# Two Transformer layers with a mixture of experts on one core: the routing step and two softmax steps put in another order

## The reference, cut to what matters

```python
x = x + softmax(layernorm_gamma_beta(sim(layernorm(x), ctx)))     # attention, layer 0
x = x + moe(layernorm(x))                                         # feed forward, layer 0
x = x + softmax(mask(scores(ctx, ctx) * layernorm(x)))            # attention, layer 1
x = x + down(silu(gate(layernorm(x))) * up(layernorm(x)))         # feed forward, layer 1

# moe: 8 experts, the best 2 of each token, at most 160 tokens of each choice for an expert
logits = xt @ gate_w;  top_p, top_i = top_k(softmax(logits), 2)
for k in range(2):
    pos = position of the token among those that chose the expert as choice k
    out += keep * w * (gelu(buf @ w1 + b1) @ w2 + b2 + gelu(buf @ wd) @ wu)
out += 0.2 * (gelu(xt @ sw1 + sb1) @ sw2 + sb2 + gelu(xt @ swd) @ swu)      # shared expert
```

## Time and profile before

| what | value |
|---|---|
| time, median of 3 runs | 301.19 us (301.11 to 302.14) |
| the profiled execution's own time | 304.5 us |
| its span | 302.7 us |
| TensorE busy | 290.1 us, 96% of the span |
| VectorE busy | 243.2 us, 80% |
| ScalarE busy | 155.2 us, 51% |
| GpSimd busy | 116.3 us, 38% |
| chain that ended last | PE 69%, DVE 11%, ACT 7%, DMA 5%, POOL 4% |

### The profile page before, as it was taken

How to read it: one execution, slowest core, us unless ns; L and a number is a source line. 1 busy time by engine, 2 the same in 40 slices (tenths; PEclk the granted TensorE clock), 3 DMA queues, 4 the chain that set the end, 5 groups by cost and what they waited for, 6 DMA issues and landing times.

```text
span 302.7 us, 5910 instructions
## 1 busy us (share of the span) xinstructions
PE 290.1 (96%) x1931; PEld 251.9 (83%) x1931; DVE 243.2 (80%) x647; ACT 155.2 (51%) x369; POOL 116.3 (38%) x144
## 2 busy tenths in 40 slices
PE   8988999969999999999999999999999899999895
PEld 6545688859898998989899888999888699999795
DVE  4888878848998988889888899898974778796733
ACT  2677985415554655646556555655533634535210
POOL 7527410351328074380834706051051215442431
PEclk9999999999999999999999999999999999999999
DMA  7933206550949448293573926446034000010102
GB/s 214 333 137 88 90 0 191 176 173 2 299 166 260 175 83 305 61 298 128 133 253 69 326 93 168 171 79 226 1 43 141 0 3 0 0 36 1 36 1 70
DMA packets 21858, 38.07 MB, mean 126 GB/s; under 512 B 3147, under 2 KB 12427, under 8 KB 21836
## 3 DMA queue, kind: packets, MB, share of 16 engines
q1 hardware_dynamic: 17356, 32.55, 32.6%
q0 software_dynamic: 4480, 5.25, 9.2%
HBM read 31.37 MB, written 6.42 MB: 125 GB/s over the span
## 4 chain that ended last, share of the span: by engine, by line
PE 69%; DVE 11%; ACT 7%; DMA 5%; POOL 4%; issue 3%; SPq 0%; DVEq 0%; POOLq 0%; ACTq 0%
PE hb L811 25%; PE yb L830 24%; PE yb L845 5%; PE hb L959 4%; PE tb L711 4%; DVE bst L1231 1%; POOL rstd L472 1%; DMA xg<-xnorm_dram,row_of 1%; DMA x<-xacc_dram 1%; DVE xn L1237 1%; PE rb L976 1%; DMA xacc_dram<-ysb,third_row 1%; PE yb L959 1%; ACT sm L1024 1%; DMA projw<-projw_dram 1%
## 5 line engine op out<-in xcount | busy, mean ns | idle before, releaser
L830 PE MATMUL yb<-raw,h 128*128 128x256 f32 x384 | 96.5, 379 | 1.4 <-ACT h L1137 1.4
L830 PEld LDWEIGHTS yb<-raw,h 128*128 128x128 f32 x384 | 69.1, 189 | 8.8 <-ACT h L1137 1.8
L1137 ACT ACTIVATE h<-hb,b 128x320 f32<-128x320 f32 (+1 forms) x80 | 44.6, 558 | 58.4 <-PE hb L811 57.1
L811 PE MATMUL hb<-xT_hi,w_hi 128*128 128x320 f32 (+1 forms) x180 | 71.2, 396 | 0.5 <-ACT small L1141 0.5
L811 PE MATMUL hb<-xT_lo,w_hi 128*128 128x320 f32 (+1 forms) x180 | 58.7, 326 | 0.0
L811 PE MATMUL hb<-xT_hi,w_lo 128*128 128x320 f32 (+1 forms) x180 | 58.6, 326 | 0.0
L573 POOL DMA_INDIRECT xacc_dram<-ysb,row_of x16 | 28.2, 1764 | 78.5 <-ACT ysb L1004 76.0
L1263 DVE COPY_PREDICATED pick<-bits,pick 128x544 int32<-128x544 uint8 x56 | 43.3, 773 | 0.6
L557 POOL DMA_INDIRECT xg<-xnorm_dram,row_of x24 | 28.7, 1196 | 32.5 <-DVE row_of L1535 16.3
L1648 DVE TENSOR_TENSOR w_lo<-raw,w_hi 128x256 fp32r<-128x256 f32 x84 | 34.5, 415 | 6.6 <-ACT w_hi L1004 6.5
L811 PEld LDWEIGHTS hb<-xT_hi,w_hi 128*128 128x128 f32 x180 | 33.9, 189 | 5.1 <-issue 2.2
(11 more groups left out here) (241 smaller groups left out, 513.5 us busy)
## 6 DMA issues: line engine op xcount, KB each, us to landing
raw<-w1pack_dram SPq DMA_DIRECT2D x30, 384.0 KB, 3.7
raw<-w2pack_dram SPq DMA_DIRECT2D x30, 384.0 KB, 5.4
idx<-idx_dram SPq DMA_DIRECT2D x8, 272.0 KB, 6.6
x<-x_dram SPq DMA_DIRECT2D x4, 256.0 KB, 4.3
xnorm_dram<-xn SPq DMA_DIRECT2D x2, 512.0 KB, 5.5
xacc_dram<-x SPq DMA_DIRECT2D x2, 512.0 KB, 8.3
x<-xacc_dram SPq DMA_DIRECT2D x4, 256.0 KB, 4.4
out_dram<-x SPq DMA_DIRECT2D x3, 256.0 KB, 2.1
```

The source lines that it names most:

```text
L811: mm = pe.matmul(hb[s % RING][:, 0:n], w[:, s, k * P:(k + 1) * P], a[:, turn, k, 0:n], start=(i == 0), stop=(i == len(terms) - 1))
L830: mm = pe.matmul(yb[c // 2][:, (c % 2) * D:(c % 2 + 1) * D], h, w, start=(s == 0 and c % 2 == 0), stop=(s == STEPS - 1), skip_group_check= ...
L1137: act.activation(hidden(s - 1, shared, turn), bank[:, 0:n], ACT.Gelu, bias=b1[:, expert, s - 1:s])\
```

## The change

Three places change. Numbers of lines from L869 on shift by one or two.

Routing: `third_slots(0)` moves on TensorE from behind the second product of step 8 to ahead of it; on VectorE `third_rows_done` moves from step 5 to step 4, and `weight_rows` from step 3 to behind it. `slot_weights` moves on TensorE from ahead of the transposes of unit 1's rows to behind them, and `weights_done` on VectorE behind the rest of those rows.

Joint: the exponentials of batch 1 move on ScalarE from between step 6 and 7 of unit 9 to behind the unit's last GELU.

Last stage, on VectorE: `finish(0)` moves from group 10 to group 11; `add_probs` of batch 3 is taken apart, one tile in group 11 and one in group 12, in place of both in group 13; `norm_x` of batch 3 moves from group 14 to group 13.

```diff
@@ PE, unit()
                             second(u, s - LAG, shared, turn, loads, range(0, 2))
                             count(1)
+                        elif s == 8:
+                            third_slots(0)
...
                         elif s == 7:
                             slot_rows(1)
-                        elif s == 8:
-                            third_slots(0)
...
             second(0, STEPS - 2, True, 0)
+            expert_rows(1, 1)
             slot_weights()
-            expert_rows(1, 1)
             second(0, STEPS - 1, True, 0)
@@ ACT
                     if u_is(u, E + 1) and s == 6:
                         exps(1, 0)
-                        exps(1, 1)
...
+            exps(1, 1)
             x3T_copy(0)
@@ DVE, unit0_extra()
                 elif s == 3:
                     rows_done()
+                elif s == 4:
+                    third_rows_done()
                     weight_rows()
-                elif s == 5:
-                    third_rows_done()
-                elif s == 8:
-                    weights_done()
...
             rows_lo(3, 1, SLOTS)
+            weights_done()
             add_shared(0)
@@ DVE, last stage
-                if f == 4 and b > 0:
+                if n == NG + 5 or f == 4 and b > 1:
                     finish(b - 1)
...
+                elif n == 11:
+                    add_probs(1, 3, 4, (0,))
+                elif n == 12:
+                    add_probs(1, 3, 4, (1,))
                 elif n == 13:
-                    add_probs(1, 3, 4)
-                elif n == 14:
                     norm_x(4, 3, x3n_ok)
```

## The result

The changed kernel takes 300.42 us (median of 10 runs, 299.7 to 306.29) against 302.25 us for the kernel before (10 runs, 301.11 to 309.08). The ratio is 0.9937, with a 95% interval of 0.9915 to 0.9958: 1.9 us faster, between 1.3 and 2.6. The prediction said 298.4 us with 297.9 to 300.2 as its range, so the sign is right, and the time lies 0.2 us outside. The three runs that the prediction started from had a median of 301.19; the ten runs, which include those three, put the kernel before at 302.25, and its profiled execution of 304.5 us lies another 2.25 above that. The profile after is of an execution of 299.7 us with a span of 298.0.

A forecast was written before the change was run, and what follows sets the result against it. TensorE, busy 96% of the span, bounds the kernel, so only its waits (gathered rows, GELU, batch 3's norm) can pay. Gains 0.7 + 0.95 + 1.1 = 2.75 us take the median 301.19 to 298.4 us; eight-in-ten range 297.9 to 300.2.

The forecast's parts named there:

- Step A: Routing before unit 1: later w1 refill lands the third gather 1.36 us sooner, map costs 0.68; gain 0.7 us.
- rival 4: Routing: the third gather comes later, so the kernel is slower, 302.8 us; chance 0.04.
- Rival 1: Routing: the gather doesn't move, its length not being the refill's doing; 299.8 us; chance 0.2.
- Step B: Joint of the layers: moving batch 1's exponentials removes TensorE's GELU wait; gain 0.95 us, bounds 0 and 1.4.
- Rival 3: Joint: a table switch holds ScalarE longer than its row, leaving a 0.3 us gain there; 299.1 us; chance 0.05.
- Step C: Last stage: batch 3's norm comes sooner and TensorE's wait for it goes; gain about 1.1 us, 0.9 to 1.3.
- Rival 2: Last stage: VectorE's standstill in group 13 eats the gain there; 299.5 us; chance 0.12.
- Rival 5: Whole kernel: change too small to see, two of three waits being the profile's own (it adds 3.3 us); 300.3; chance 0.11.

The follow-up runs named there:

- same_third: The kernel before with no edit, profiled and timed again; ratio to before 0.9987 (0.9951 to 1.0022).
- hold: Kernel before, with SyncE asking for the w1 refill only when unit 1's gathered rows have landed; ratio to before 1.0001 (0.9971 to 1.003).
- third_only: Kernel before with the third chunk's rows and `weight_rows` moved, the weights map left ahead of the transposes; ratio to before 1.001 (0.9979 to 1.0042).
- joint: Kernel before with only batch 1's exponentials moved behind the last GELU on ScalarE; ratio to before 0.9946 (0.9915 to 0.9976).
- best: Changed kernel with the weights map back ahead of the transposes and batch 3's norm left in group 14; ratio to before 0.9893 (0.9854 to 0.9931).
- routing: Kernel before with only the routing edits on TensorE and VectorE; ratio to before 0.9993 (0.995 to 1.0035).
- same: The kernel before with no edit, profiled and timed anew; ratio to before 1.0029 (0.999 to 1.0067).
- same_again: The kernel before with no edit, a further sample of its executions; ratio to before 0.9989 (0.995 to 1.0027).
- map_only: Kernel before with only the weights map moved behind the transposes, the refill as early as before; ratio to before 1.0029 (0.9983 to 1.0074).
- third_again: The third_only version against the kernel before, timed and profiled again; ratio to before 0.9995 (0.9955 to 1.0034).
- after_map_first: Changed kernel with only the weights map put back ahead of the transposes; ratio to before 0.9947 (0.9918 to 0.9976).
- after_fourth: The whole change with no further edit, timed and profiled again; ratio to before 0.992 (0.9888 to 0.9951).
- after_again: The whole change with no further edit, timed and profiled again; ratio to before 0.9947 (0.9916 to 0.9979).

## Why the prediction was wrong

**The anchor.** "The median 301.19 becomes 298.4" took three runs for the kernel's time. Ten gave 302.25. That is 1.06 of the 2.0 us by which the forecast missed. In the experiments, on four chips, the kernel before was timed mostly between 300.6 and 305 us, with many runs near 300.9, 302.4 and 304. The range had no term for this: moved up by 1.06 it would be 299.0 to 301.3 and would hold 300.42. The other 0.9 us is gain that didn't come, 1.9 in place of 2.75, and most of that is step A.

**Step A, "A gains 0.7 us", is the term of the sum that failed.** Its edit did what was said: refill at 62.29 (forecast near 62), map behind the transposes, no cost for the early copy of the third rows, no gather later (rival 4). What failed is its premise that the 4.3 us gather and the 2.5 us wait are the kernel's. They come when GpSimd starts 1.0 to 1.1 us behind `row_of`, in two profiles (before, same_third). In the others the third gather takes 2.5 to 2.9 us with the refill early, late or held, and there is nothing to win from the refill: hold timed 1.0001. Timed, A is worth 0.3 us plus or minus 0.8 by itself, and third_only nothing plus or minus 0.8, so the timings don't tell a small gain from a small loss. The text of the forecast also puts the refill "between" the second and the third gather; by its own rows (60.86 against 60.38) it stands behind the third. Rival 1 ("the gather doesn't move", 299.8) comes nearest to this mechanism.

**Step B, "B gains 0.95", was right for its execution and too large for others.** The working holds: no GELU wait, covered exponentials, the norm late next. But x's return belongs to the execution: 4.2 to 4.8 us or about 3.1. The gain is 0.9 with the one and 0.4 with the other, so the single 0.95 should have been 0.4 to 0.9. The forecast's own sign of being wrong, `gate_up` of group 0 less than 0.5 us sooner from reading x back, is met where x comes back early in both kernels (17.78 to 17.39 or 17.41); the 1.5 us between the profiles of before and after are mostly x's return. Joint alone was timed at 1.6 us plus or minus 0.9.

**Rival 3 fell.** Each of ScalarE's three loads up to the moved exponentials (from 231.07, 233.66 and 237.30 in after) takes 1.28 us; it starts 0.01 to 0.02 us behind the activation before it, and the next one starts 0.01 to 0.02 behind the load. The rule of the Trainium skill (ScalarE: Activation LUTs, What ACT_TABLE_LOAD costs) with its 1.38 us of drain isn't seen in the records here.

**Step C, "about 1.1", was right and a little small.** Group 0 to the end went from 57.3 or 57.4 to 55.9 or 56.0 in every profile with C as in the change, whatever the execution: 1.35 to 1.4, with 1.3 as the forecast's upper value. VectorE stood still for 1.83 us as forecast. Rival 2 ("the standstill eats C") fell: it costs only the 0.2 to 0.3 us that best gets back.

**The sum.** B between 0.4 and 0.9 and C at 1.35 give 1.8 to 2.3 us, and the whole change measured 2.0 plus or minus 0.4: little or nothing is left for A. The forecast's own bounds were also added up too low: A from 0, B from 0.7 and C from 0.9 give 1.6 us, so 299.6 and not 299.1. Rival 5 named 300.3, next to the measured 300.42, with the wrong reason. The change is seen clearly in the timings; the waits that were missing from other runs are one of the three, not two; and the 3.3 us aren't what a profile adds: 304.5 us is within the spread of the kernel's timings, and the profiled execution of after, 299.7 us, is itself the lowest of its ten runs.

**What stays open.** In the profiles A shortens `row_of` to unit 1 by 0.9 us (10.7 to 9.8), which with B and C would make 2.6 us or more of the change, and third_only shortens it by 1.4; the timings (2.0 plus or minus 0.4, and nothing plus or minus 0.8) exclude both as a rule for all runs. In the routing order of before the copy starts 9.1 to 9.5 us behind `row_of` in every profile, also where the transposes ended 2 us earlier (next section). By the pieces of the table a run of the kernel before near 300.9 us needs about 9.2 us to unit 1; with 10.7 and x back early it takes 302.4. No kept profile of that order has 9.2. The timings hint at where to look: beside the profiles with the late copy, on two chips, none of 80 timed runs of the kernel before was under 302.0 us, while in 90 on the two other chips 11 were under 301.1. So the delay may be in most runs of some chips and missing from some runs of others, and A may gain on the one and lose on the other. That isn't shown: routing on the first of these chips timed 0.9993.

## What to carry to other kernels

A wait in one profile is a sample: before pricing its removal, ask which transfer ends it and how far that transfer's time varies (in the profile's own table of durations, or in a second profile of the same kernel), and price the removal at both ends. Cut two profiles at instructions that both have; the pieces that differ although the code is the same measure the executions, here 1.6 us at x's return and at least 1.6 at the gather (4.3 against at most 2.7), each nearly the whole gain. And list all that an engine waits for ahead of a late step: GpSimd's second condition, the write of the rows that it gathers, explains its lateness here and stood in the first trace. Engine work in series (C, from the exponentials through two sums and a norm) could be summed to 0.25 us, while the term that ended in a gather's landing (1.36 us sooner) wasn't there at all in most executions.

## What the runs showed of the hardware

TensorE's results can be seen late. In hold the transposes start at 62.56 and take 1.18 us, and TensorE's next matmuls follow at 63.67, but ScalarE's copy, which has nothing else to wait for, starts at 65.66. VectorE sees it too: in same it stands idle for 2.9 us and reads the weights map (L1542) 3.3 us behind the map's last matmul, within 0.1 us of ScalarE's copy. The same gap of about 2 us is in same, same_again, joint and last, on two chips, and of 1.2 to 1.3 us in both profiles of best. It was not in the profiles of before, same_third, routing, map_only, third_again, after_map_first or any of the changed kernel: there the copy starts 0.03 to 0.04 us behind the transposes. The order of the program isn't enough to bring it: best and after_map_first have the same order up to here, 1.2 us in the one and 0.03 in the other. Nor is the refill, which hold keeps back. But all five gaps of 2 us are in the routing order of before, and none of the profiles with the map behind the transposes has a gap. In the profiles with the delay the records of some semaphore updates nearby are missing too, the gathers' landings among them, but so they are in routing and after_fourth, which have no delay. What the delay is stays open.

The same read of x from memory, at the same place, takes 3.0 to 3.4 us or 4.2 to 4.8 us until the first batch is there, and nothing between; both came with the changed kernel. Only the first batch is late: the fourth landed 5.0 us after its issue in after and 5.2 in after_again. The Trainium skill (DMA: Bandwidth & Descriptors, Latency and other measured facts) gives HBM's access latency as 0.2 us on average and 2 us at high load, which would be enough for this difference; no run here shows that it is the cause.
